# Attention output by a centred projection, rows normalised from PSUM, and the steps behind it moved ahead: a fused state-space, attention and expert kernel

## What is computed

```
x = x + ss2d(group_norm(x))                  # depthwise conv, selective scan (256 channels x 16 states)
t = tokens(x)                                # 2304 rows of 128 per image
t = t + attention(ln_t(t))                   # linear attention, 8 heads of 16
t = t + experts(ln_t(t))                     # 8 experts, each row goes to its top 2, silu(h) * g

def attention(x):
    x = layer_norm(x, norm_gamma); q, k, v = split(x @ w_qkv.T)
    q = softmax(q, over features) * scale;  k = softmax(k, over tokens)
    out = (q @ (k.T @ v)) @ w_out.T          # per head, then the projection
    return layer_norm(out, out_gamma)        # (out - mean) * rsqrt(var + 1e-5) * out_gamma
```

## Time and profile before

| | |
|---|---|
| runs | 3912.74, 3913.9, 3920.4 us |
| the profiled execution's own time | 3908.72 us |
| its span in the profile | 3906.9 us |
| PE, DVE, ACT, POOL busy | 81%, 76%, 65%, 74% |
| eight scans, from the start of one to the next | 355, 371, 421, 438, 444, 440, 438, 421 us |
| tail behind the last scan | 3416.1 to 3906.9 us |

### The profile page before, as it was taken

How to read it: one execution, slowest core, us unless ns; L and a number is a source line. 1 busy time by engine, 2 the same in 40 slices (tenths; PEclk the granted TensorE clock), 3 DMA queues, 4 the chain that set the end, 5 groups by cost and what they waited for, 6 DMA issues and landing times.

```text
span 3906.9 us, 68984 instructions
## 1 busy us (share of the span) xinstructions
PE 3163.4 (81%) x17390; PEld 2012.8 (52%) x17390; DVE 2983.4 (76%) x5234; ACT 2553.7 (65%) x6158; POOL 2909.4 (74%) x3055
## 2 busy tenths in 40 slices
PE   5687888778889888988889887988889888776772
PEld 3233354335556555655556555655556555566662
DVE  3698989988898888878897788888898788822110
ACT  3455677457867777676867777676867777665451
POOL 1465757686769886888868897888968887966755
PEclk9788999789989998999989999999989999988896
DMA  3965656465869677886869677886869677856773
GB/s 89 221 146 129 157 124 162 120 161 137 221 177 263 153 211 197 222 221 163 233 178 244 158 208 194 231 212 162 231 185 260 157 202 195 235 150 182 241 233 109
DMA packets 420323, 730.02 MB, mean 187 GB/s; under 512 B 56203, under 2 KB 313814, under 8 KB 417750
## 3 DMA queue, kind: packets, MB, share of 16 engines
q1 hardware_dynamic: 302422, 484.13, 49.7%
q10 hardware_dynamic: 99072, 203.47, 17.0%
q0 software_dynamic: 18432, 37.93, 3.5%
HBM read 596.93 MB, written 100.07 MB: 178 GB/s over the span
## 4 chain that ended last, share of the span: by engine, by line
PE 24%; POOL 22%; issue 21%; DVE 15%; ACT 11%; DMA 4%; ACTq 2%; SPq 1%; POOLq 1%; DVEq 0%; PEldq 0%
POOL prod L698 10%; DVE state L1582 6%; PE ps_conv L901 5%; PE ps_main L967 4%; DVE ps_x L1569 3%; POOL got L821 3%; PE ps_g L1085 2%; DMA dt_rep<-dt_dram 2%; POOL rows_in L798 2%; PE ps_g L1092 2%; POOL hidden L810 2%; PE ps_y L981 2%; ACT dt_rep L1206 2%; PE ps_h L1073 2%; PE ps_x L915 1%
## 5 line engine op out<-in xcount | busy, mean ns | idle before, releaser
L698 POOL TENSOR_TENSOR prod<-state,c_rep 128x384 f32<-128x384 f32 x1536 | 1532.7, 1007 | 608.5 <-DVE state L1582 588.7
L1582 DVE TENSOR_TENSOR_SCAN state<-dt_rep,carry,ps_x 128x384 f32<-128x384 f32 x1280 | 1285.8, 1005 | 0.0
L1569 DVE TENSOR_TENSOR ps_x<-ps_x,db_rep 128x384 f32<-128x384 f32 x1536 | 852.9, 555 | 243.0 <-PE ps_x L915 223.7
L1206 ACT ACTIVATE dt_rep<-dt_rep,vecs 128x384 f32<-128x384 f32 x1536 | 917.8, 615 | 137.9 <-DMA dt_rep<-dt_dram 77.7
L915 PE MATMUL ps_x<-x_stack,copy 96*128 96x384 bf16 x1536 | 534.2, 350 | 310.8 <-DVE state L1582 306.4
L901 PE MATMUL ps_conv<-gx,w_conv 128*128 128x384 f32 x1728 | 689.6, 507 | 8.0 <-DVE parts L1599 4.6
L915 PEld LDWEIGHTS ps_x<-x_stack,copy 96*128 96x128 bf16 x1536 | 153.9, 100 | 681.6 <-DVE state L1582 493.1
L1390 ACT ACTIVATE g_sb<-ps_g,w_down 128x128 f32<-128x128 f32 x1032 | 304.2, 371 | 231.1 <-PE ps_g L1092 226.3
L901 PEld LDWEIGHTS ps_conv<-gx,w_conv 128*128 128x128 f32 x1728 | 301.1, 195 | 216.6 <-issue 129.6
L1073 PE MATMUL ps_h<-u_t,w_up 128*128 128x128 f32 x2064 | 327.5, 298 | 104.0 <-DVE silu L1799 80.0
L810 POOL TENSOR_TENSOR hidden<-g_sb,silu 128x384 f32<-128x384 f32 x344 | 343.7, 999 | 83.9 <-ACT u_out L1396 74.8
(11 more groups left out here) (256 smaller groups left out, 4958.7 us busy)
## 6 DMA issues: line engine op xcount, KB each, us to landing
dt_rep<-dt_dram SPq DMA_DIRECT2D x384, 768.0 KB
w_up<-in_w_exp ACTq DMA_DIRECT2D x344, 384.0 KB
w_down<-in_w_exp ACTq DMA_DIRECT2D x344, 193.5 KB
x_stack<-parts SPq DMA_DIRECT2D x576, 48.0 KB
u_in<-rows_in SPq DMA_DIRECT2D x344, 64.5 KB
rows_out<-u_out SPq DMA_DIRECT2D x344, 64.0 KB
dt_dram<-dt SPq DMA_DIRECT2D x192, 96.0 KB
qv<-in_x SPq DMA_DIRECT2D x48, 192.0 KB
```

Source lines behind the costliest of these rows:

```text
L698: pool.tensor_tensor(prod[:, k % HS, :], state[:, k % HS, :], c_rep[:, c % 2, :], ALU.mult).then_inc(s_prod.sem, 1)
L1206: act.activation(dt_rep[:, g % XS, q, :], dt_rep[:, g % XS, q, :], ACT.Exp, scale=decay_rate).then_inc(s_decay.sem, 1)
L1569: dve.tensor_tensor(x_n, x_n, db_rep[:, c % 2, :], ALU.mult).then_inc(s_inflow.sem, 1)
L1582: dve.tensor_tensor_scan(state[:, k % HS, :], dt_rep[:, g % XS, q, :], ps_x[k % XB][:, 0:T], init, ALU.mult, ALU.add).then_inc(s_state.sem, 1)
```

## The change

The projection's weight `w_proj` becomes two matrices side by side: at setup DVE subtracts each row's mean over the outputs, and a second copy is multiplied by `out_gamma`. `ctx2` and `ctx_o` are thus 256 columns wide, and one matmul a tile gives centred rows and centred rows times gamma. The uses `ao0` to `ao5` are replaced by `ap0` to `ap8` of two tiles each. ACT does not evacuate them: it squares the centred half from PSUM with a sum along the row (into a scratch), takes Ln and Exp of two columns (the reciprocal root), and DVE multiplies the gamma half in PSUM by it and adds t in one SCALAR_TENSOR_TENSOR, in place in `acc`. DVE's BN_STATS of that group follows one step later. Gone are the copy of `ao` on ACT, one normalisation with its statistics, POOL's work between, one root, and POOL's multiplication by gamma and addition.

`acc` is now `u_tok` rather than `q_tok`, so t is reloaded at step 66 instead of 81, and is stored in two parts at steps 79 and 87. What follows stands nine to ten steps sooner: rows normalised from step 92, the choice of experts at 110 to 121, lists at 123 to 127, scatters from 137 at one in two steps (15/8 before), the next image's x loaded from 98 and turned from 113 to 130. The experts' tiles begin at step 280 rather than 273, eight `AMONG` the others and the rest from 320, closer together.

```diff
-SEQ2 = ("qT0", "qT1", "ao0", "qT2", "ao1", "qT3", "ao2", "qT4", "ao3", "qT5", "ao4", "ao5")
-T_SEQ2 = 68
-T_AGAIN, T_STAT2, T_NORM2, T_STAT3 = 81, 82, 86, 98
-T_GAMMA = tuple(87 + g + g // 2 for g in range(NC))
...
+T_QT, T_AP = (64, 66, 67, 71, 75, 79), (68, 69, 72, 73, 76, 77, 80, 81, 83)
+NA = NT // 2
+T_AGAIN, T_STAT2 = 66, 88
+T_ACC = (79, 87)
...
-AMONG = (81, 84, 87, 90, 93, 96, 99, 102, 107, 112, 119, 126, 132)
-T_AMONG, T_LAST = 137, 220
+AMONG = (88, 91, 94, 98, 103, 110, 117, 122)
+T_AMONG, T_LAST = 128, 220
...
-T_SCATTER = tuple(146 + 15 * k // 8 for k in range(NT)) + tuple(183 + 15 * k // 8 for k in range(NT))
...
+T_SCATTER = tuple(137 + 2 * k for k in range(NT)) + tuple(177 + 2 * k for k in range(NT))
...
-        w_proj = sb("w_proj", [P, D])
-        out_gamma = sb("out_gamma", [P, D])
+        w_proj = sb("w_proj", [P, 2, D])
...
-        ctx_t, ctx_o = sb("ctx_t", [P, D]), sb("ctx_o", [P, D])
+        ctx_t, ctx_o = sb("ctx_t", [P, D]), sb("ctx_o", [P, 2 * D])
...
-        acc = x_in = q_tok
+        acc, x_in = u_tok, q_tok
...
                 elif w.j is not None:
-                    due(sp, s_accout, w.j, 1)
-                    apart()
-                    due(sp, s_xn, w.j, 3 * NC)
+                    sp.wait_ge(*full(w.j, f"qT{NC - 1}"))
...
-                    sp.wait_ge(*full(m, "qT5"))
+                    sp.wait_ge(*full(m, "ctx"))
                     apart()
-                    sp.dma_start(acc.rearrange("p k d -> p (k d)"), image_rows(t1_dram, m)).then_inc(s_t1in.sem, 16)
-                if t == T_STAT3 - 1:
-                    due(sp, s_acc, m, NC)
-                    sp.dma_start(image_rows(acc_dram, m), acc.rearrange("p k d -> p (k d)")).then_inc(s_accout.sem, 16)
+                    sp.dma_start(acc, image_rows(t1_dram, m).rearrange("p (k d) -> p k d", d=D)).then_inc(s_t1in.sem, 16)
+                for half, (first, last) in enumerate(((0, 10), (10, NT))):
+                    if t == T_ACC[half]:
+                        for x in (f"ap{last // 2 - 1}", f"ap{last // 2 - 2}"):
+                            sp.wait_ge(*read(m, x))
+                            apart()
+                        sp.dma_start(image_rows(acc_dram, m)[:, D * first:D * last].rearrange("p (k d) -> p k d", d=D),
+                                     acc[:, first:last, :]).then_inc(s_accout.sem, 16)
...
-                for g in range(NC):
-                    tiles = slice(TT * g, TT * g + TT)
-                    if t == T_GAMMA[g]:
-                        due(pool, s_xn, m, NC + g + 1)
-                        pool.tensor_tensor(k_tok[:, tiles, :], k_tok[:, tiles, :],
-                                           out_gamma[:, :].unsqueeze(1).broadcast_to([P, TT, D]), ALU.mult).then_inc(s_gam.sem, 1)
-                    if t == T_GAMMA[g] + 1:
-                        due(pool, s_gam, m, g + 1)
-                        due(pool, s_t1in, m, 2)
-                        pool.tensor_tensor(acc[:, tiles, :], acc[:, tiles, :], k_tok[:, tiles, :], ALU.add).then_inc(s_acc.sem, 1)
...
-                elif kind == "ao":
-                    for x in other_bank(name, "ctx2", f"qT{g}"):
+                elif kind == "ap":
+                    for x in other_bank(name, "ctx2", f"qT{2 * g // TT}", f"qT{(2 * g + 1) // TT}"):
                         pe.wait_ge(*read(m, x))
-                    for k in range(TT):
-                        ins = pe.matmul(o[:, P * k:P * k + P], turned[:, T * g + P * k:T * g + P * k + P], ctx_o[:, :],
-                                        start=True, stop=True)
+                    for k in range(2):
+                        r = P * (2 * g + k)
+                        ins = pe.matmul(o[:, 2 * D * k:2 * D * k + 2 * D], turned[:, r:r + P], ctx_o[:, :], start=True, stop=True)
                 elif kind == "uT":
...
-                    pe.matmul(aux("ctx2", m)[:, 0:D], ctx_t[:, :], w_proj[:, :], start=True, stop=True).then_inc(fills("ctx2", m), 1)
+                    pe.matmul(aux("ctx2", m)[:, 0:2 * D], ctx_t[:, :], w_proj[:, :, :].rearrange("p a d -> p (a d)"), start=True, stop=True).then_inc(fills("ctx2", m), 1)
...
-                elif kind == "ao":
-                    evacuate(m, name, big_k[:, T * g:T * g + T], o)
+                elif kind == "ap":
+                    logs()
+                    act.wait_ge(*full(m, name))
+                    tiles = slice(2 * g, 2 * g + 2)
+                    for k in range(2):
+                        t = 2 * g + k
+                        ins = act.activation(k_tok[:, t, :], aux(name, m)[:, 2 * D * k:2 * D * k + D], ACT.Square, accum_out=mv[:, t, 0:1])
+                    ins.then_inc(s_square.sem, 1)
+                    due(act, s_square, m, g + 1)
+                    act.activation(mv[:, tiles, 1], mv[:, tiles, 0], ACT.Ln, bias=eps_ln, scale=1.0 / D).then_inc(s_aln.sem, 1)
+                    due(act, s_aln, m, g + 1)
+                    act.activation(r2[:, tiles], mv[:, tiles, 1], ACT.Exp, scale=-0.5).then_inc(s_rms.sem, 1)
...
-                if 0 <= t - T_NORM2 < NC:
-                    normalise(m, 1, t - T_NORM2, k_tok, k_tok)
-                if t == T_STAT3 + 1:
-                    root(m, 4, mv[:, :, 1], r1[:, :])
-                if t in T_NORM3:
-                    if t == T_NORM3[0]:
-                        act.wait_ge(*full(m, "ctx"))
-                    normalise(m, 2, T_NORM3.index(t), acc, u_tok)
+                if t in T_NORM2:
+                    if t == T_NORM2[0]:
+                        due(act, s_accout, m, 2)
+                    normalise(m, 1, T_NORM2.index(t), acc, u_tok)
...
+            sums, means = gmv[:, 0:1], gmv[:, 1:2]
+            dve.tensor_reduce(sums, w_proj[:, 0, :], AX.X, ALU.add).then_inc(s_centre.sem, 1)
+            dve.wait_ge(s_centre.sem, 1)
+            dve.tensor_scalar(means, sums, -1.0 / D, None, ALU.mult).then_inc(s_centre.sem, 1)
+            dve.wait_ge(s_centre.sem, 2)
+            dve.tensor_scalar(w_proj[:, 0, :], w_proj[:, 0, :], means, None, ALU.add).then_inc(s_centre.sem, 1)
+            dve.wait_ge(s_centre.sem, 3)
+            dve.tensor_tensor(w_proj[:, 1, :], w_proj[:, 0, :], prod[:, 4, 0:D], ALU.mult).then_inc(s_setup.sem, 1)
...
-            def row_stats(m, src, g):
-                for t in range(TT * g, TT * g + TT):
-                    ins = dve.bn_stats(st[:, t, :], src[:, t, :])
-                if g == NC - 1:
+            def add_rows(m, a):
+                name = f"ap{a}"
+                if a == 0:
+                    due(dve, s_t1in, m, 2)
+                due(dve, s_rms, m, a + 1)
+                for k in range(2):
+                    t = 2 * a + k
+                    ins = dve.scalar_tensor_tensor(out=acc[:, t, :], in0=aux(name, m)[:, 2 * D * k + D:2 * D * k + 2 * D],
+                                                   scalar=r2[:, t:t + 1], in1=acc[:, t, :], op0=ALU.mult, op1=ALU.add)
+                ins.then_inc(frees(name, m), 1)
+            def row_stats(m, a):
+                dve.wait_ge(*read(m, f"ap{a}"))
+                for t in (2 * a, 2 * a + 1):
+                    ins = dve.bn_stats(st[:, t, :], acc[:, t, :])
+                if a == NA - 1:
                     ins.then_inc(s_stats.sem, 1)
...
                     dve.wait_ge(*full(m, "ctx2"))
-                    dve.tensor_scalar(ctx_o[:, :], aux("ctx2", m)[:, 0:D], k_col[:, 3:4], DH ** -0.5, ALU.mult, ALU.mult).then_inc(frees("ctx2", m), 1)
-                for g in range(NC):
-                    if t == T_SEQ2 + SEQ2.index(f"ao{g}") + 2:
-                        dve.wait_ge(*read(m, f"ao{g}"))
-                        row_stats(m, k_tok, g)
-                for g in range(NC):
-                    if t == T_GAMMA[g] + 3:
-                        due(dve, s_acc, m, g + 1)
-                        row_stats(m, acc, g)
+                    dve.tensor_scalar(ctx_o[:, :], aux("ctx2", m)[:, 0:2 * D], k_col[:, 3:4], DH ** -0.5, ALU.mult, ALU.mult).then_inc(frees("ctx2", m), 1)
+                for a in range(NA):
+                    if t == T_AP[a] + 2:
+                        add_rows(m, a)
+                    if t == T_AP[a] + 3:
+                        row_stats(m, a)
```

63 lines of the change are left out of this document (33 added, 30 removed).

## The result

The changed kernel is slower: 3992.9 us (median of 4 runs, 3991.4 to 3995.2) beside 3913.3 us of the kernel before, a ratio of 1.0205 (95% interval 1.0183 to 1.0227). I had forecast 3895 and a range of 3852 to 3926.

What follows compares the result with a forecast made beforehand. No engine bounds the whole; each stretch was read alone. Seven passes (-10.5), tail (-10) and setup (+1.3) took 3908.7 to 3889.5 us; with 5.2 from execution to median, 3895 us, range 3852 to 3926.

Steps and rivals of the forecast that it cites:

- Experts' tiles: Step 144 to the pass's end: 3.6 us more PE work, half counting, +1.7 us a pass, bounds 0 and +3.5.
- Steps 80 to 111: Relief of POOL (-11), ACT (-13) and DVE (-2.8) partly passed on: -4.5 us a pass, between 0 and -8.0.
- POOL near 54 us: Sign expected in steps 80 to 111: POOL's busy time near 54, with the stretch at 69 to 70 us.
- Steps 112 to 151: Routing's DVE work moves from 128 to 143 into 112 to 127: -1.7 us a pass, bounds -3 and +1.
- Steps 64 to 79: DVE, the bound there, gains 2.9 us of work: +3.0 us a pass, bounds 1.5 and 6.
- The reload: t loaded at step 66, needed at 70: 6.5 us for a 7.7 us load; carried by the upper bound of 6.
- rival (3): Slower: reload lands late, DVE waits at step 70, +4 to +5 us a pass, 3927 us; chance 0.15.
- Prices: Per instruction: DVE addition 290 ns, Square 0.28 to 0.47 us, Ln and Exp 214 ns; 18 wider matmuls +2 us.
- The tail: After the scans: gamma work and tiles leave, table loads come; -10 us taken, bounds -20 and +4.
- Setup: Kernel's start: four dependent small DVE operations come in, about +1.3 us with the waits between them.
- (1): Rival: relief counts in full, steps 80 to 111 fall to PE's 66.1 us; 3853 to 3859 us; chance 0.23.
- (2): Rival: it comes out even, moved DVE work costs as much as it saves; about 3916 us; chance 0.22.

Runs made afterwards that it cites:

- e2: Changed kernel with 13 experts' tiles among attention's work and the rest from step 137, spaced 2.68 steps as before: 3907.0 us, ratio 0.9975.
- e5: Kernel before with the changed kernel's tile steps from 138 on and without its tile at 132, nothing else: 3970.4 us, ratio 1.0162.
- e9: Changed kernel with three tile steps one earlier (138, 140, 143 to 137, 139, 142): 3961.9 us, ratio 1.0110.
- e1: Changed kernel's arithmetic with nearly all that follows (rows, choice, turning, scatters, gathers, tiles) back at the old steps: 3935.3 us, ratio 1.0050.
- e7: Kernel before without POOL's multiplication by out_gamma (output lacks gamma): 3899.4 us, ratio 0.9967.
- e6: Kernel before with its 32 evenly spaced tiles each one step later, the last still at 220: 3931.2 us, ratio 1.0048.

## Why the prediction was wrong, step by step

- *The step that failed*: "Experts' tiles ... stand 2.56 steps apart ... half of it counts: +1.7, bounds 0 and +3.5". I took the table as an amount of PE work in a stretch. In the median of four passes steps 144 to 191 cost 12.5 us more than before; beside e2, with the tiles' old spacing, it is 9.8, and 5.3 more in 128 to 143 and 3.8 in 0 to 63. For these last two stretches the term for the tiles had nothing. What counts is which of the scan's steps a tile meets: a Tanh behind the two table loads of the softplus, a product late on DVE, the next tile waiting at the head of PE's queue with the scan behind it. e2 (-86), e5 (+60 in the old kernel) and e9 (-31 for three entries) show it. The upper bound of +3.5 had no row under it, though PE's waits for `silu` stood in part 5 of the page of the kernel before: 80.0 us of idle time before PE's L1073 over the whole span (134.7 after, before L1068).
- *Steps 80 to 111*, -4.5 "a little over the middle": measured -3.0 in the pass shown and -1.7 in the median of four, with six tiles beginning there for nine. I had POOL near 54 us, and it came to 60.4 even so, because the change also moves six of the 18 gathers from steps 102 to 117 to steps 78 to 102, which neither my account of the change nor the prediction has: 12 gathers stand in this stretch for 6. In e1, with nine tiles and the gathers where they were, POOL is at 51.7 (65.5 before) and ACT at 58.9 (64.6), and the stretch takes 74.4 for 74.1. So in a full pass the relief of the two busiest engines was not passed on. Without experts it was in part: -4.5 in e1's second pass, where DVE (42.2 of 44.6 us before) lost 3.7. e7 fits some relief by POOL (11 us in all, half of it in the tail), and doesn't show in which stretch.

```profile
2316.09:2390.52 74.43, 62.19 (x361) 39.88 (x360) 60.12 (x104) 58.91 (x156) 51.73 (x59) 0.98 0.81 216
```

- *Steps 112 to 151*, -1.7: DVE's work moved about as I had it (36.1 for 31.2, +4.9 with +5.9 forecast, and 37.4 for 45.3, -7.9 with -5.5 forecast), but 112 to 127 took 4.8 longer, where I had let 2.2 to 4 us count, and 128 to 143 only 0.6 less. I had taken the last pass's 4.9 us as the price of DVE's work; in the changed kernel the wait of 5.1 us took the place of it. Without it (e9) steps 128 to 143 come to 42.8 in the median of four passes, near the 43 forecast.
- *Steps 64 to 79*, +3.0: measured +1.3 in this pass and +2.4 in the median of four, so this term held for the full passes (+1.4 if one goes on to step 87). The second pass, which I priced like the others, is another matter: its steps 64 to 87 took 7.5 us more, with 5.3 us more of work on DVE, the bound there.
- *The reload and rival (3)*: DVE did not wait for the load in the scans. The load was issued at 2325.11, DVE's first addition stands at 2334.09, and no wait of DVE there is put down to the load. Slower was right in rival (3), but for another reason than the rival's.
- *Prices*: DVE's addition from PSUM took 340 ns for the 290 taken, Ln 296 for 214 and Exp 203, Square with its read 273 + 203 = 476, just above the 280 to 470 taken, PE 412 for 294 (2.1 us for 18, with 2 taken). The table loads a pass are 17 for 19, as forecast. They were right enough, and mattered little.
- *The tail*, -10: +0.5. From `ctx_o` to the offsets -9.2 (-7 forecast), the stage behind +8.8 (+3.5 forecast), scatters and rest -3.4 (-6), and +4.3 ahead of `ctx_o`, which I hadn't priced and whose cause no run shows: the last images' tiles are run out there at the new table's pace, but e5, with nearly the same table, has no longer tail.
- *Setup*: +3.4 for +1.3; the start varies from 88.2 to 94.4 us over these kernels, so this is not resolved.
- *Rivals*: none named the tiles' place. (1) is excluded by e1, where steps 80 to 111 stay at 74.4 for the 66.1 that it needs. (2), about 3916, comes near e2 (3907.0, ratio 0.9975), not the kernel as it was changed.

What stays open: why some of the other places cost what they do. For 172 to 183 e5 shows that the loss goes with the tiles' steps. For 144 to 147 the runs disagree: they take 11.1 us before, 13.9 in the changed kernel and 13.3 in e5, but also 13.1 in e2, where the tiles from 137 on stand at their old steps. And in the last pass, which has no next image, the changed kernel's tile steps lose nothing (steps 144 to 190 take 87.8 us, 89.9 before), while in e5 they do (95.2). Only the place of 12 to 15 and 140 to 143 was followed to its wait.

## What to carry to other kernels

Where one in-order engine serves two streams, a table of the second stream's steps is not only an amount of work but a choice of places in the first stream's period. In the kernel before, a change of spacing from 83/31 to 92/36 of a step cost 60 us without adding any work (e5), and one step of shift at the same spacing cost 20 (e6). Before moving a table of steps, mark on the first stream's period where its function tables are changed and its long instructions stand, and ask of each entry what it would wait for at that place, rather than summing busy time by stretch. And busy shares of 85% on all engines do not say which relief will count: in e1's full pass 14 us less of GpSimd and 6 less of ScalarE left steps 80 to 111 as long as they were.

## What the runs showed of the hardware

The same VectorE TENSOR_SCALAR (128 x 2304, SBUF to SBUF) took 1.46, 2.82 and up to 6.15 us, with GpSimd's instructions beside it; it got no turn between GpSimd instructions that follow one another without a gap (4.7 us of them), and when it began first it was GpSimd's that grew (2.48 for 1.80 us in the changed kernel). A PE kept waiting for 5.1 us came back at half speed: 1.64 us for six matmuls that took 0.83 before the wait, at a granted clock of 0.50 (1.2 GHz) for 1.00.
